# Two-layer graph network on one core: a new order for ScalarE's copies in layer 0's projection stage

## The reference, cut to what matters

```python
def layer0(x, src, dst):
    x_l = x @ W_l.T + b_l
    agg = segment_sum(x_l[src], dst)
    out = agg / maximum(deg, 1.0)[:, None] + x @ W_r.T
    return layernorm(x + out)        # (v - mean) / sqrt(var + 1e-5)
```

## Time and profile before

| | |
|---|---|
| Median of three runs | 2965.13 us (2956.29 to 2967.65) |
| The profiled execution | 2964.21 us; its span is 2962.5 us |
| Busy shares over the span | TensorE matmuls 79%, VectorE 76%, GpSimd 66%, ScalarE 47% |
| The stage | first `mean` at 1352.86 us, last line 1060 at 1603.64 us |

### The profile page before, as it was taken

The page is one execution under the profiler, slowest core; times in us unless marked ns, Lnnn a source line. Parts: engine busy times, 40 slices in busy tenths (PEclk is TensorE's granted clock), DMA queues, the critical chain, the costliest instruction groups (busy, mean ns, idle before and its releaser), DMA issues.

```text
span 2962.5 us, 53780 instructions
## 1 busy us (share of the span) xinstructions
PE 2333.3 (79%) x9888; PEld 1014.9 (34%) x9888; DVE 2242.3 (76%) x4956; ACT 1402.1 (47%) x3557; POOL 1953.1 (66%) x2021
## 2 busy tenths in 40 slices
PE   3288988898999989887886677777777777776996
PEld 1133444444444444433332232223222323222443
DVE  6899888888888888886876666666665666654998
ACT  3501555656555555553344443443443443442776
POOL 0277777777777777772112777777777777775775
PEclk8699999999999999999998989888898898875998
DMA  5577777777877777775456888888888888878676
GB/s 202 174 203 230 229 225 226 234 229 235 236 223 234 231 222 232 232 214 148 148 162 210 247 244 252 249 242 252 248 244 249 250 241 252 248 218 182 226 241 202
DMA packets 247012, 664.11 MB, mean 224 GB/s; under 512 B 39593, under 2 KB 40423, under 8 KB 246949
## 3 DMA queue, kind: packets, MB, share of 16 engines
q0 software_dynamic: 144640, 475.92, 56.6%
q1 hardware_dynamic: 101828, 186.19, 18.5%
q10 hardware_dynamic: 480, 1.28, 0.2%
HBM read 573.26 MB, written 89.97 MB: 224 GB/s over the span
## 4 chain that ended last, share of the span: by engine, by line
PE 37%; DVE 19%; DMA 19%; issue 13%; POOL 5%; DVEq 4%; ACT 1%; POOLq 0%; SPq 0%; ACTq 0%
PE ps L1139 36%; DMA rows<-table,idx_ring 16%; POOL rows L542 4%; DVE acc L897 3%; DVE acc L977 3%; DVE onehot L884 2%; DVEq L891 2%; DVE where L909 2%; POOL rows L526 1%; DMA table<-rows 1%; DMA g_idx<-table,idx_ring 1%; DVE flat L1094 1%; DVE flat L1047 1%; DVE st L1051 1%; DVE flat L1049 1%
## 5 line engine op out<-in xcount | busy, mean ns | idle before, releaser
L1139 PE MATMUL ps<-rows,onehot 128*128 128x512 f16 (+1 forms) x4104 | 896.3, 335 | 365.8 <-DMA rows<-table,idx_ring 172.9
L526 POOL DMA_INDIRECT rows<-table,idx_ring x928 | 894.4, 964 | 309.3 <-issue 211.8
L977 DVE TENSOR_TENSOR acc<-acc,ps 128x513 f32 x880 | 606.4, 689 | 440.9 <-PE ps L1139 301.1
L1139 PEld LDWEIGHTS ps<-rows,onehot 128*128 128x128 bf16 x4104 | 371.6, 102 | 933.5 <-issue 220.3
L542 POOL DMA_INDIRECT rows<-table,idx_ring x440 | 422.9, 961 | 150.5 <-issue 95.4
L1139 PE MATMUL ps<-where,put 128*128 128x440 bf16 x1664 | 451.0, 353 | 37.9 <-DVE where L909 36.6
L1139 PE MATMUL ps<-w_b,flat 128*128 128x512 f32 x784 | 470.1, 684 | 0.0
L909 DVE TENSOR_SCALAR where<-iota_chunk,cw_ring 128x880 bf16<-128x880 f16 x832 | 428.1, 515 | 8.6 <-PE ps L1139 1.7
L1448 ACT ACTIVATE put<-spot,flat 128x128 f16<-128x128 f16 x832 | 265.7, 390 | 337.5 <-PE ps L1139 330.2
L1436 ACT ACTIVATE spot<-iota_node,flat 128x128 f16<-128x128 f16 x832 | 340.4, 479 | 125.5 <-DVE flat L753 125.5
L897 DVE TENSOR_TENSOR acc<-acc,ps 128x513 f32 x464 | 318.3, 686 | 97.1 <-PE ps L1139 55.1
(11 more groups left out here) (236 smaller groups left out, 2335.4 us busy)
## 6 DMA issues: line engine op xcount, KB each, us to landing
table<-rows SPq DMA_DIRECT2D x98, 257.0 KB, 3.7
rows<-table,idx_ring POOLq DMA_INDIRECT x1368, 3.9
xr_scratch<-edges SPq DMA_DIRECT2D x49, 256.0 KB
rows<-xr_scratch SPq DMA_DIRECT2D x49, 256.0 KB, 3.2
h_scratch<-rows SPq DMA_DIRECT2D x49, 256.0 KB, 2.1
flat<-h_scratch SPq DMA_DIRECT2D x49, 256.0 KB, 5.1
hb_scratch<-spot SPq DMA_DIRECT2D x49, 256.0 KB, 4.1
u_scratch<-flat SPq DMA_DIRECT2D x49, 256.0 KB
```

Of the source, the lines that this page charges most:

```text
L526: nc.gpsimd.indirect_dma_start(out=rows[:, k % GB, :], out_offset=None, in_=tables[layer][:, :], in_offset=bass.IndirectOffsetOnAxis(ap=id ...
L977: V.tensor_tensor(tile_acc, tile_acc, part, ALU.add).then_inc(s_acc, 1)
L1139: return nc.tensor.matmul(*args, skip_group_check=True, **kw)
```

## The change

ScalarE's steps for tile t, `tile(t, k)`, come in another order. Before, they are: `high_half(t - 1)`, `mean(t + 2)`, `turned(t + 1)`, root of t. After, they are: `turned(t + 1)`, `mean(t + 2)`, `high_half(t - 1)`, root of t. No instruction is added or removed, and each keeps its own waits.

```diff
             def tile(t, k):
+                if not (isinstance(t, int) and t + 1 >= T):
+                    turned(t + 1, k + 1)
+                if not (isinstance(t, int) and t + 2 >= T):
+                    mean(t + 2, k)
                 if not (isinstance(t, int) and t == 0):
                     high_half(t - 1, k + 1)
-                if not (isinstance(t, int) and t + 2 >= T):
-                    mean(t + 2, k)
-                if not (isinstance(t, int) and t + 1 >= T):
-                    turned(t + 1, k + 1)
                 act.wait_ge(s_var, t + 1)
                 nc.scalar.activation(sd[:], mv[:, 1:2], ACT.Sqrt, bias=eps[:]).then_inc(s_sd, 1)
```

## The result

The changed kernel takes 2934.89 us (median of four runs, 2932.57 to 2935.77), the kernel before 2961.68 (four runs, 2956.29 to 2967.65). The ratio is 0.9908, 95% interval 0.9888 to 0.9927: 26.8 us faster. The forecast was 2947.5 with a range from 2938 to 2958. One execution of a kernel further down (`old_spread`, 3736 us at a granted clock of 0.555) is slow where all others are fast, and is left out.

A forecast was written before the change was run, and what follows sets the result against it. Taken as bound: the two-tile loop through ScalarE's queue. Opening 2.2, decode periods 7.1 and the remaining tiles 8.3 us sum to 17.6 off 2964.21, giving 2946.6, or 2947.5 against the runs' median; range 2938 to 2958.

The forecast's parts named there:

- The turn: Loop of two tiles through ScalarE's queue, from line 1047 to line 1047 two tiles on: 9.20 us falls to 8.18.
- The root's follower: In ScalarE's queue, turned starts 0.25 us after the root starts; bounds 0.20 and 0.30.
- to X 3.73: Link from the projection's start to the start of line 1047 two tiles on, taken as 3.73 us.
- TensorE's own limit: TensorE, projection to transposes 3.53 us and on to projection 0.49: 4.02 a tile, 8.04 for two.
- Opening: Stage start, line 1047 of tile 0 to that of tile 4: 2.2 us less.
- Decode periods: Seven four-tile periods, tiles 4 to 32, with VectorE's edge-list decodes: 1.02 us less each, 7.1 in all.
- X(32) to X(47): Line 1047 of tile 32 to that of tile 47, free of decodes: 8.3 us less.
- The clock: TensorE's clock falls behind some stalls, 1.4 to 2.1 us each: four falls again, no difference.
- Rival 1: TensorE's clock falls at every stall, four more falls costing 6.8 us: gain 10.8, 2954 us; chance 0.20.
- Rival 2: TensorE's clock falls only at the long stall, three falls fewer giving 5.1 us: 2942.5 us; chance 0.15.
- The stores: Line 1060 waits for table stores two tiles back; landing 3.3 us, deciding from 4.03. As the bound: 2958 us, chance 0.08.
- Q: Experiments' theory: the new queue order shortens the stage's two-tile loop, and that is the whole effect, about 19 us.

The follow-up runs named there:

- old_spread: Kernel before, ScalarE's old order kept, with the decodes cut into 48 pieces spread behind the tiles: 2943.33 us, ratio 0.9951.
- mean_first: Kernel before with only the mean moved ahead of the high half in ScalarE's queue: 3480.18 us, ratio 0.9976 on a slower chip.
- turned_only: Kernel before with only turned moved to the head of ScalarE's queue: 3488.20 us, ratio 0.9996 on a slower chip.
- after_third: The changed kernel, unchanged, timed again against the kernel before on a faster chip: 2939.33 us, ratio 0.9948.

## Why the prediction was wrong

**What bounds the kernel: right.** The loop through the queue order was the bound, and mean_first and turned_only give its turn as its links say, to 0.02 us.

**The turn: the mechanism right, two terms off.** I had 8.18 us, it is 8.02. The root's follower came after 0.20, not 0.25, which is what the Trainium skill's "ScalarE: Activation LUTs" gives (section "What ACT_TABLE_LOAD costs", an overlap of about 93 ns); here the trace agrees, 0.29 long and the next one 0.20 behind. turned to mean was 0.47, not 0.50. The largest part is "to X 3.73": it is 3.64 when the projection doesn't also wait for turned. In the old order the copy ended only 0.06 before the projection, and I took the row's length over without asking what else had held it. What I called TensorE's own limit, 8.04 for two tiles, came from rows of the old order too, and the new turn is already below it. In the rows after the change TensorE goes from a projection to the next transposes in 3.43 and on to the next projection in 0.44, which is 3.87 a tile and 7.74 for two. So the loop through ScalarE still bounds the stage. By these rows a better order of its queue, say with the mean ahead of the root, could win up to 0.28 a turn and not just another 0.14 (an estimate; no kernel tried it).

**The sum over the stage: right to 1.3 us, from terms that are off both ways.**
- Opening, 2.2 forecast, 4.2 measured (20.22 to 16.05): the clock did not fall there, and TensorE was idle for 1.74 us where I had 2.4.
- Decode periods, 7.1 forecast, 5.5 measured (144.31 to 138.78): the four falls of the changed kernel cost some 7.2 us in them (an estimate by the form of the prediction), against 5.5 before. Without the falls 7.2 is left.
- X(32) to X(47), 8.3 forecast, 9.2 measured (70.15 to 60.93): the shorter turn.

Together 18.9 against 17.6.

**The clock: the number right, the rule behind it not known.** Four falls, as forecast, in the profiles of the result and of the two repeats on faster chips, but six on the slower chip, which accounts for its 221.9 us. They were not the four that I took over: the opening and the first decode are not among them, the sixth and the seventh are. The kernel before itself has four falls in one profile and three in the two others. So that the count came out is in part luck. Idle time alone does not decide it. TensorE's rows at two stalls of the changed kernel:

```profile
1397.57 0.66 PE L1341 MATMUL ps<-ident,flat 128*128 128x128 f32 x4 [2.30 <-ACT flat L1473]
1398.06 3.60 PE L1139 MATMUL ps<-w_a,flat 128*128 128x512 f32 x8
...
1440.27 0.66 PE L1341 MATMUL ps<-ident,flat 128*128 128x128 f32 x4 [1.98 <-ACT flat L1473]
1440.76 5.30 PE L1139 MATMUL ps<-w_a,flat 128*128 128x512 f32 x8
```

After 2.30 us it stayed at 2.4 GHz, with a granted clock of 1.00 from 1397 to 1403 us; after 1.98 it fell, with 0.72 from 1440 to 1446. Rival 1 (all eight) and rival 2 (only the long one) did not come. With the decodes in pieces the falls behind the opening were gone.

**The stores: right.** The landing of the table's store went from 3.3 (at most 3.8) to 3.5 (at most 4.2); in after_third it stayed at 3.3 (at most 3.9). With the turn at 8.02 the store decides from 3.87 on, not from 4.03, and most landed sooner. The estimate of 1.8 us more, from the Trainium skill's "DMA: Bandwidth & Descriptors" (section "Latency and other measured facts"), was not borne out: the median rose by 0.2 at most.

**The step that failed: from the stage to the time.** The prediction put everything outside the stage at nothing ("X(0) is set by a load and does not move", "the shift is kept to the end"), took the median of three runs as its base, and moved the range by 3 us for the noise of both ("runs of one kernel spread 11 us (2956 to 2968), which moves the lower end to 2938"). The time came 12.6 us below the forecast, and this is where they lie:
- The base: 2965.13 with three runs, 2961.68 with the fourth, 3.4 us.
- The stage: 18.9 for 17.6, 1.3 us.
- Outside the stage: 26.8 less 18.9, 7.9 us, put at nothing. In the two profiles X(0) came 9.2 us earlier and the rest behind X(48) was 3.6 shorter.

The whole-time comparisons say 26.8, 19.1, 15.5 and 19.7 us. Three agree with Q within their intervals, the first does not. The forecast's 17.6 lies inside all three repeats. The medians of the kernel before in the repeats on faster chips are 2954.8 and 2955.7, some 6 us under the 2961.68 of the first comparison, while the changed kernel's 2934.89 is 1 and 4 us under its repeats. So most of what the first comparison has too much lies with the kernel before, of which it has four runs. With hindsight, a range of 2930 to 2958 would have covered it. What made the first comparison differ is not settled: the code ahead of the stage is the same, the repeats do not show the 8 us again, and no run here singles it out.

## What to carry to other kernels

In an in-order queue, put first what the next tile needs, and last what waits for this tile's end; then write the loop down, one duration for each link, and ask of each duration whether a second wait is hidden in it. Work of another engine's queue that comes in a lump between two tiles gives back a part of what a tighter loop wins, because the lump is measured against less slack. Cutting the lumps to the size of the slack gave 16 to 19 us more in the stage here (16 in the whole time, on the chip where both were run), nearly as much as the order itself. And take the base of a forecast from as many runs as the gain needs: with a gain of 18 us and runs that spread 11, three or four of each kernel were too few.

## What the runs showed of the hardware that was not expected

- The same kernel took 2955 to 2962 us in three comparisons (two chips, and one whose number isn't known) and 3491 on two other chips, while this stage took the same on both kinds. The difference lies in the gather phases, 278 us ahead of X(0) and 255 behind X(48). There, between 600 and 1000 us, VectorE's add of line 897 waited 33.5 us for 156 instructions on a faster chip and 100.5 us for 127 on a slower one. The mean granted clock was 0.90 to 0.92 on the faster kind and 0.84 to 0.86 on the slower. What is cause and what is consequence is not shown.
- TensorE's clock fell after an idle time of 1.98 us and not after one of 2.30, in the same run. The places were the same ones (the third, fourth, sixth and seventh decode) in three runs of the changed kernel on faster chips. In the kernel before it fell at the first decode after 2.02 us in one run and after 2.01 in another, and not after 2.01 at the same place in a third.
- An addition on VectorE that takes 0.69 us took 0.92 on average when a copy on GpSimd had begun before it, and the copy took 0.99 instead of 0.62 when the addition had begun first (old_spread and the kernel before).
